# Macaron block on one core: a scratch field cleared behind each scatter of routed rows, TensorE's expert numbers as steps of their own, and newly written orders

## The reference, cut to what matters

```python
x = x + 0.5 * int8_linear(layernorm(x))             # quantised by token, weight int8
x = x + griffin_block(layernorm(x))                 # rmsnorm, conv, RG-LRU scan, gate; then a gated FFN of 512
x = x + 0.5 * int8_linear(layernorm(x))
x = x + 0.5 * moe(layernorm(x))                     # shared expert + top 2 of 8 experts, inner size 256
x = x + gated_linear_attention(layernorm(x))        # state 128x128 a sequence
x = x + 0.5 * moe(layernorm(x))                     # the same weights

def moe(x):                                         # expert: (silu(x Wg) * (x Wu)) Wd
    scores, idx = top_k(sigmoid(x Wr + rb), 2)
    out = shared(x)
    for e in range(8): out += cw[..., e] * expert_e(x)
```

## Time and profile before

| | |
|---|---|
| runs, us | 683.24, 683.96, 685.11 (median 683.96) |
| span of the profiled execution, us | 692.3 |
| mean granted clock of TensorE | 0.972 |
| instructions | 14370 |
| busy, us | PE 600.1, PEld 476.3, DVE 497.2, ACT 387.7, POOL 419.3 |
| POOL's scatters (L840) | 128.1 us in 128 |
| POOL's tile stores (L1132) | 96.3 us in 98 and 43.7 us in 44 |

### The profile page before, as it was taken

How to read it: one execution, slowest core, us unless ns; L and a number is a source line. 1 busy time by engine, 2 the same in 40 slices (tenths; PEclk the granted TensorE clock), 3 DMA queues, 4 the chain that set the end, 5 groups by cost and what they waited for, 6 DMA issues and landing times.

```text
span 692.3 us, 14370 instructions
## 1 busy us (share of the span) xinstructions
PE 600.1 (87%) x4124; PEld 476.3 (69%) x4124; DVE 497.2 (72%) x1721; ACT 387.7 (56%) x1019; POOL 419.3 (61%) x445
## 2 busy tenths in 40 slices
PE   0366999999989998999897899999999999978974
PEld 0224565655666797888696686769879989857863
DVE  7997999978998865557224798989877766553335
ACT  2395968988766545444353728466565355533541
POOL 5276696488567777567643614553776575775552
PEclk9996999999999999999999999999999999999997
DMA  7999000001033355666768600124216556566796
GB/s 258 410 411 371 0 1 1 1 0 32 13 99 94 97 156 161 186 193 180 211 176 245 235 6 1 35 66 131 74 43 172 153 151 177 161 182 189 231 297 232
DMA packets 60125, 100.97 MB, mean 146 GB/s; under 512 B 10288, under 2 KB 28592, under 8 KB 59792
## 3 DMA queue, kind: packets, MB, share of 16 engines
q1 hardware_dynamic: 50832, 81.52, 38.5%
q0 software_dynamic: 8640, 17.84, 7.4%
q10 hardware_dynamic: 576, 0.69, 0.3%
HBM read 61.79 MB, written 38.23 MB: 144 GB/s over the span
## 4 chain that ended last, share of the span: by engine, by line
PE 43%; DVE 13%; DMA 9%; issue 6%; POOL 3%; SPq 2%; ACT 2%; POOLq 0%; DVEq 0%; ACTq 0%
PE bank L1083 13%; PE bank L1058 6%; PE bank L1296 5%; DMA tin<-rows_by_expert 3%; PE bank L969 3%; PE bank L955 3%; PE bank L944 2%; DMA hid<-rows_done 2%; DMA rows_done<-tout,tdst 2%; PE bank L1064 2%; DMA rows_done<-tout,tin 1%; POOL rows_by_expert L840 1%; DVE qt L417 1%; PE bank L312 1%; PE bank L307 1%
## 5 line engine op out<-in xcount | busy, mean ns | idle before, releaser
L840 POOL DMA_INDIRECT rows_by_expert<-xx,sidx x128 | 128.1, 1001 | 72.2 <-issue 34.0
L1083 PE MATMUL bank<-tint,twt 128*128 128x128 f32 x1136 | 151.8, 282 | 6.0 <-DVE thidt L1121 3.4
L1083 PEld LDWEIGHTS bank<-tint,twt 128*128 128x128 f32 x1136 | 141.1, 196 | 22.0 <-issue 12.3
L1132 POOL DMA_INDIRECT rows_done<-tout,tin x98 | 96.3, 983 | 57.5 <-ACT tout L1107 34.8
L1121 DVE TENSOR_TENSOR thidt<-tsil,bank 128x256 f32<-128x256 f32 x142 | 58.2, 418 | 95.8 <-ACT tsil L1099 74.1
L1099 ACT ACTIVATE tsil<-bank 128x256 f32<-128x256 f32 x142 | 53.9, 384 | 89.9 <-PE bank L1083 88.4
L1058 PE MATMUL bank<-e_dn,thidt 128*128 x568 | 90.6, 286 | 15.5 <-DVE thidt L1121 7.3
L1058 PEld LDWEIGHTS bank<-e_dn,thidt 128*128 128x128 f32 x568 | 76.8, 195 | 25.2 <-issue 24.8
L1107 ACT ACTIVATE tout<-bank,tin 128x128 f32<-128x128 f32 x142 | 50.2, 366 | 62.9 <-PE bank L1064 43.7
L1132 POOL DMA_INDIRECT rows_done<-tout,tdst x44 | 43.7, 993 | 49.0 <-ACT tout L1107 35.9
L1296 PEld LDWEIGHTS bank<-bufA,bufB 128*127 128x127 f32 (+6 forms) x448 | 47.7, 176 | 11.6 <-issue 6.7
(11 more groups left out here) (272 smaller groups left out, 1331.0 us busy)
## 6 DMA issues: line engine op xcount, KB each, us to landing
twt<-moe_gu SPq DMA_DIRECT2D x142, 256.0 KB
rows_by_expert<-tout SPq DMA_DIRECT2D x25, 715.0 KB, 20.0
tin<-rows_by_expert SPq DMA_DIRECT2D x142, 65.0 KB, 2.6
hid<-rows_done SPq DMA_DIRECT2D x12, 512.0 KB, 5.5
x<-x_in SPq DMA_DIRECT2D x8, 256.0 KB, 4.4
rows_by_expert<-xx,sidx POOLq DMA_INDIRECT x128
out<-x SPq DMA_DIRECT2D x8, 256.0 KB, 3.9
rows_done<-tout,tin POOLq DMA_INDIRECT x98
```

The lines of the kernel that those rows point to most:

```text
L840: pool.indirect_dma_start(out=rows_by_expert, out_offset=bass.IndirectOffsetOnAxis(ap=sidx[h][:, k:k + 1], axis=0), in_=xx[h][:, r, t, :], ...
L1083: m = pe.matmul(bank[UP_BANKS[p][j]][:, c * P:(c + 1) * P], weights[:, c * P:(c + 1) * P], tint[g % TURNS][:, :], start=True, stop=True)
L1132: pool.indirect_dma_start(out=rows_done, out_offset=bass.IndirectOffsetOnAxis(ap=dst, axis=0), in_=tout[:, g % RING, :], in_offset=None).t ...
```

## The change

Three things. First, a scratch tile `pause` of 128 x 112 floats is cleared behind each of the 128 scatters, and POOL waits for the end of that; there is nothing of the kind behind the 142 tile stores. Second, the wait for the table and the register reads of TensorE leave `x_io_tensor` and become a step `x_ids_tensor`, called 38 times. Third, the five orders are written anew; apart from `x_ids_tensor` they have the same steps as before (sync 315, vector 636, gpsimd 293, scalar 745, tensor 704 and now 742).

```diff
 LEVELS = 7
+PAUSE = 112
 PIECES = 3
...
         tdst = sb("tdst", [P, RING], I32)
+        pause = sb("pause", [P, PAUSE])
         tout = sb("tout", [P, RING, P])
...
                     ap=sidx[h][:, k:k + 1], axis=0), in_=xx[h][:, r, t, :], in_offset=None).then_inc(s_scat[h], 16)
+                pool_step(pool, pool.memset(pause[:, :], 0.0))
 
 
...
+        def x_ids_tensor(pe, p, j):
+            pe.wait_ge(s_table, WAVES * p + wave_of(j) + 1)
+            expert_pe.update(values_of(ENG.PE, etab[p], chunk_at(j), E_ROUTED))
+
...
             if s >= LAG_DOWN:
                 j = s - LAG_DOWN
                 g = p * NT + j
-                if chunk_at(j):
-                    pe.wait_ge(s_table, WAVES * p + wave_of(j) + 1)
-                    expert_pe.update(values_of(ENG.PE, etab[p], chunk_at(j), E_ROUTED))
                 pe.wait_ge(s_thid, g + 1)
                 for c in range(IJ):
                     m = pe.matmul(bank[b][:, P:2 * P], thidt[g % TURNS][:, c, :], e_dn[:, expert_pe[j], c, :],
```

POOL's order at the start:

```diff
             k_first_gpsimd(pool)
             q_root1_gpsimd(pool, 0)
             q_root1_gpsimd(pool, 1)
+            k_split_gpsimd(pool)
             q_bias_gpsimd(pool, 0, 0)
-            k_split_gpsimd(pool)
             q_bias_gpsimd(pool, 1, 0)
             f_root_gpsimd(pool, 0)
             q_root_gpsimd(pool, 1, 0)
+            f_rstd_gpsimd(pool, 0)
             q_root_gpsimd(pool, 2, 0)
+            f_apply_gpsimd(pool, 1)
             q_bias_gpsimd(pool, 2, 0)
             q_bias_gpsimd(pool, 3, 0)
-            f_rstd_gpsimd(pool, 0)
-            f_apply_gpsimd(pool, 1)
             f_apply_gpsimd(pool, 0)
+            q_bias_gpsimd(pool, 4, 0)
             f_b_gpsimd(pool, 0)
             f_root_gpsimd(pool, 1)
             f_b_gpsimd(pool, 1)
+            f_root2_gpsimd(pool, 0)
...
```

DVE's order at the start:

```diff
             q_mom1_vector(dve, 0)
             q_stats_vector(dve, 1, 0)
             q_limits_vector(dve, 1, 0)
-            q_mom1_vector(dve, 1)
             q_par1_vector(dve, 0)
             q_scale_vector(dve, 0, 0)
             k_first_vector(dve)
+            q_whole_vector(dve, 0, 0)
+            q_mom1_vector(dve, 1)
+            q_limits_vector(dve, 3, 0)
+            q_stats_vector(dve, 2, 0)
             q_par1_vector(dve, 1)
+            k_decay_vector(dve)
             q_scale_vector(dve, 1, 0)
-            q_whole_vector(dve, 0, 0)
+            q_out_vector(dve, 0, 0)
             q_whole_vector(dve, 1, 0)
+            q_stats_vector(dve, 3, 0)
             q_limits_vector(dve, 2, 0)
-            q_limits_vector(dve, 3, 0)
-            q_out_vector(dve, 0, 0)
-            q_stats_vector(dve, 3, 0)
             f_stats_vector(dve, 0)
-            q_stats_vector(dve, 2, 0)
             q_out_vector(dve, 1, 0)
+            q_stats_vector(dve, 4, 0)
             f_stats_vector(dve, 1)
...
```

SP's order at the end:

```diff
+            for j in range(69, 71):
                 t_load_sync(sp_, 1, j)
-            t_weights_sync(sp_, 1, 66)
+            for j in range(68, 71):
+                t_weights_sync(sp_, 1, j)
             t_stored_sync(sp_, 1, 0)
             c_fetch_sync(sp_, 0, 1)
-            for j in range(68, 71):
-                t_load_sync(sp_, 1, j)
-            for j in range(67, 70):
-                t_weights_sync(sp_, 1, j)
             c_fetch_sync(sp_, 1, 1)
             c_fetch_sync(sp_, 2, 1)
-            t_weights_sync(sp_, 1, 70)
             c_fetch_sync(sp_, 3, 1)
             c_fetch_sync(sp_, 4, 1)
             c_fetch_sync(sp_, 5, 1)
             t_stored_sync(sp_, 1, 6)
             c_fetch_sync(sp_, 6, 1)
+            t_stored_sync(sp_, 1, 7)
+            c_fetch_sync(sp_, 7, 1)
             o_store_sync(sp_, 0)
             o_store_sync(sp_, 1)
             o_store_sync(sp_, 2)
-            t_stored_sync(sp_, 1, 7)
-            c_fetch_sync(sp_, 7, 1)
             o_store_sync(sp_, 3)
             o_store_sync(sp_, 4)
             o_store_sync(sp_, 5)
...
```

TensorE's order around the first tile of pass 1's last wave (an excerpt; `x_io_tensor(1, 49)` transposes it):

```diff
             x_up_tensor(pe, 1, 44)
-            x_io_tensor(pe, 1, 48)
+            e_gate_tensor(pe, 7, 1, 0)
+            x_ids_tensor(pe, 1, 41)
             x_up_tensor(pe, 1, 45)
-            x_io_tensor(pe, 1, 49)
+            for j in range(46, 49):
+                x_io_tensor(pe, 1, j)
             x_up_tensor(pe, 1, 46)
-            x_io_tensor(pe, 1, 50)
+            x_ids_tensor(pe, 1, 45)
+            e_up_tensor(pe, 7, 1, 0)
+            x_ids_tensor(pe, 1, 49)
             x_up_tensor(pe, 1, 47)
+            for j in range(49, 51):
+                x_io_tensor(pe, 1, j)
+            for j in range(48, 50):
...
```

More of the change, by code:

```diff
@@ L1534, in _ @@
                 t_load_sync(sp_, 0, j)
-            for j in range(31, 36):
+            for j in range(32, 35):
                 t_weights_sync(sp_, 0, j)
@@ L1555, in _ @@
                 t_load_sync(sp_, 0, j)
-            for j in range(47, 51):
+            for j in range(47, 49):
                 t_weights_sync(sp_, 0, j)
@@ L1659, in _ @@
             for j in range(44, 47):
                 t_load_sync(sp_, 1, j)
-            for j in range(41, 45):
+            for j in range(43, 48):
                 t_weights_sync(sp_, 1, j)
@@ L2448, in _ @@
             g_bias_gpsimd(pool, 1)
-            for j in range(65, 67):
-                t_store_gpsimd(pool, 0, j)
             g_root_gpsimd(pool, 1)
@@ L2455, in _ @@
             g_root_gpsimd(pool, 2)
+            for j in range(64, 67):
+                t_store_gpsimd(pool, 0, j)
             r_scatter_gpsimd(pool, 0, 1, 0)
@@ new lines, in _ @@
+            x_io_tensor(pe, 0, 24)
+            r_counts_tensor(pe, 6, 0)
+            e_up_tensor(pe, 5, 0, 0)
+            e_gate_tensor(pe, 5, 0, 1)
+            e_up_tensor(pe, 5, 0, 1)
+            for j in range(23, 25):
+                x_up_tensor(pe, 0, j)
+            x_io_tensor(pe, 0, 25)
+            e_down_tensor(pe, 5, 0)
+            r_turn_tensor(pe, 7, 0)
+            x_ids_tensor(pe, 0, 21)
+            x_ids_tensor(pe, 0, 25)
+            x_io_tensor(pe, 0, 26)
+            r_logits_tensor(pe, 7, 0)
@@ new lines, in _ @@
+            x_io_tensor(pe, 0, 39)
+            e_down_tensor(pe, 6, 0)
+            x_up_tensor(pe, 0, 39)
+            for j in range(40, 43):
+                x_io_tensor(pe, 0, j)
+            x_up_tensor(pe, 0, 40)
+            e_gate_tensor(pe, 7, 0, 0)
+            e_up_tensor(pe, 7, 0, 0)
+            x_io_tensor(pe, 0, 43)
+            x_up_tensor(pe, 0, 41)
+            x_ids_tensor(pe, 0, 53)
+            for j in range(42, 44):
+                x_up_tensor(pe, 0, j)
+            x_io_tensor(pe, 0, 44)
@@ L3107, in _ @@
             e_down_tensor(pe, 5, 1)
+            x_ids_tensor(pe, 1, 29)
             x_up_tensor(pe, 1, 27)
-            x_io_tensor(pe, 1, 29)
+            for j in range(29, 31):
+                x_io_tensor(pe, 1, j)
             r_turn_tensor(pe, 6, 1)
@@ new lines, in _ @@
+            x_up_tensor(pe, 1, 63)
+            for j in range(65, 67):
+                x_io_tensor(pe, 1, j)
+            x_up_tensor(pe, 1, 64)
+            x_ids_tensor(pe, 1, 65)
+            for j in range(67, 69):
+                x_io_tensor(pe, 1, j)
+            for j in range(65, 67):
+                x_up_tensor(pe, 1, j)
+            x_io_tensor(pe, 1, 69)
+            x_up_tensor(pe, 1, 67)
+            for j in range(70, 72):
+                x_io_tensor(pe, 1, j)
+            x_up_tensor(pe, 1, 68)
@@ L3589, in _ @@
-            x_in_scalar(act, 0, 67)
+            for j in range(53, 55):
+                x_out_scalar(act, 0, j)
+            x_silu_scalar(act, 0, 56)
+            x_in_scalar(act, 0, 59)
+            for j in range(55, 57):
+                x_out_scalar(act, 0, j)
+            for j in range(60, 62):
+                x_in_scalar(act, 0, j)
+            for j in range(57, 60):
+                x_silu_scalar(act, 0, j)
+            x_out_scalar(act, 0, 57)
+            for j in range(62, 65):
+                x_in_scalar(act, 0, j)
```

2001 lines of the change are left out of this document (982 added, 1019 removed).

## The result

The changed kernel takes 703.8 us (median of 4 runs, 703.16 to 705.52) against 683.6 before: ratio 1.0295, 95% interval 1.0275 to 1.0315, 20 us slower. I had forecast 686.5 with a range up to 698. The direction was right, the size was not.

What follows compares the result with a forecast made beforehand. TensorE, busy 87% of the span, was taken as the bound, with POOL nearly full where waves wait for scatters. Start -4.5, pass 0 +8.5, register loads -2.5, pass 1 +4.6, end -3.5 gave +2.6 us: 686.5, range 675 to 698.

Steps and rivals of the forecast that it cites:

- start: First 62 us: apply(1) fills POOL's idle stretch and b(0) comes earlier, -4.5 us (bounds -5.8 and -1).
- pause, pass 0: Units 2 to 7 of pass 0: 0.30 us per scatter, 0.61 before a store, 17.7 us before absorption.
- pause, pass 1: Units 6 and 7 of pass 1: pauses plus one store, less 0.3 idle, +4.6 us (bounds +1 and +7).
- new order in pass 0: Units 2 to 7: two more tile stores ahead of POOL's last scatter, 1.26 us each, +2.5.
- register loads: Chunk heads on PE: expert-number reads come earlier, behind matmuls already queued, -2.5 us (bounds 0 and -6).
- end: Last tiles: all loads issued first and c_adds put behind x_hid(70), -3.5 us (bounds -5 and -1).
- Of this the 10.0 us of idle time is absorbed: Pass 0, units 2 to 7: POOL's idle time takes up 10.0 of 20.2 us added; +8.5 reaches the last wave.
- elsewhere the pause costs nothing: Units 0, 1 of pass 0 and 0 to 5 of pass 1: POOL idles while PE works, so no cost.
- signs named ahead: In the new trace: scatters 1.56 us start to start, unit 7's last at about 339, PE idle time growing.
- cheap pause (0.08): POOL's scatters: the 0.30 gap overlaps the memset, pause nearly free, start and end pay; 675.6 us, chance 0.31.
- half price: POOL's scatters: 0.20 us each, pass 0 +5, pass 1 +3.5; 682 to 684 us, chance 0.13.
- fourth rival: Register loads still stop PE's queue, the next engine holds the start (-1); sum +8.6, 692.5 us, chance 0.07.

Runs made afterwards that it cites:

- e6: Kernel before with the new order only up to the first scatter of unit 0 (some 155 us), no pause: 683.39 us, ratio 0.9962.
- e5: Kernel before with the pause added behind the 64 scatters of pass 0 only: 695.4 us, ratio 1.0164.
- e11: Kernel before with the pause added behind the 64 scatters of pass 1 only: 690.15 us, ratio 1.0086.
- e7: Kernel before with the new order only from some 155 to 430 us (pass 0), no pause: 696.84 us, ratio 1.0167.
- e2: Changed kernel without the pause's memset and its wait; new orders and register steps stay: 699.77 us, ratio 1.0236.
- e8: Kernel before with the new order only from some 628 us to the end, no pause: 683.74 us, ratio 0.9967.
- e4: Changed kernel with TensorE's register reads put back into x_io, pause and orders kept: 707.44 us, ratio 1.0336.
- e1: Kernel before, unchanged, run again for a second trace: 684.88 us, ratio 1.0016.
- e3: Kernel before with only the pause added behind all 128 scatters: 705.65 us, ratio 1.0310.
- e9: New order in pass 0 only, no pause, with the last wave's table moved behind x_hid(0, 33) on DVE: 691.89 us, ratio 1.0113.

## Why the prediction was wrong, step by step

| step of the sum | forecast | measured on the 684 us chips |
|---|---|---|
| start | -4.5 | -2.6 (-0.5 to -4.7), e6 |
| pause, pass 0 | +6.0 (8.5 less two stores) | +11.2 (7.9 to 14.5), e5 |
| pause, pass 1 | some +5 | +5.9 (3.8 to 8.0), e11 |
| new order in pass 0 | +2.5 (two stores) | +11.4 (8.6 to 14.4), e7 |
| new order in pass 1 | some -0.5 | some +10 (2 to 18) if the parts add, what e2 leaves over e6, e7 and e8; not run alone |
| register loads | -2.5 | not settled, e4 |
| end | -3.5 | -2.3 (-0.2 to -4.3), e8 |
| all | +2.6 | +20 |

Two steps failed.

**The first is "Of this the 10.0 us of idle time is absorbed".** It was wrong twice. The 10.0 came from one slow execution; the second trace has 5.1 (e1). And that idle time was not room for more work: in e3 POOL's line of work grew by 12.7 us, its idle time beyond the fixed gaps stayed (5.1 and 5.6 us), and the stretch grew by 13.0. The reading that fits is that POOL, the ring of slots, the loads and PE form a loop. Without the absorption my own price per pause would have given 17.7 in pass 0; the true one gives 12.7 for the old order, and by e5 11.2 of that is in the time.

**The second is what I gave no price**: the rewritten middle of the orders. I compared the place of each x_io in PE's work and found it the same within some 5 us, and let "apart from two stores" stand for nothing. That comparison doesn't see what stands ahead of a short step on another engine. All new orders and register steps together were forecast at -8.5 us (-4.5, +2.5, -0.5, -2.5, -3.5) and cost 16 without the pause (e2). The table of the last wave, 6 us of DVE, moved from behind x_hid(34) to ahead of x_hid(30), which cost 3.7 us (e9, 0 to 7). Of the rest of pass 0's 11.4, the wait for tile 65's load (3.2 us against 0.8) is the longest single wait in the trace and was not tested; pass 1's share was not found on a chip where it counts. e2's trace has one candidate there: PE waits 5.05 us at 621.3 for a thidt behind the last table of pass 1, which in the old order stands one x_hid later.

**Where it was right.** The start gained by the mechanism named: apply(1) fills POOL's idle stretch (36.58 in the changed kernel), b(0) starts at 49.66 instead of 53.13, and mix(0) waits 1.24 us at 55.12 instead of 5.77 at 56.47. At mix(0) itself 1.3 us show, for DVE is the next to be late, as feared; in the changed kernel unit 7's FFN ends at 226.7 us, where e1 has 226.2, and in e6 the first tile's transposition is 0.8 us earlier than in e1 (208.00 against 208.79). So the median's 2.6 is only in part followed through the trace. POOL's timeline there:
```profile
36.58 3.14 POOL L621 TENSOR_SCALAR h<-x,lf_mean,lf_rstd 128x128 f32<-128x128 f32 x4
...
49.66 1.45 POOL L591 TENSOR_TENSOR bufB<-bufD,bufB 128x512 f32<-128x512 f32 x1
```
The end gained as described: the c_add at 682.88 waits for nothing (5.45 us before). Pass 1's pause came out near its price, but not where I had it: "elsewhere the pause costs nothing" is wrong, since e11 lost some 4.4 us before the last waves begin. The sign of the whole was partly luck: the pause cost less on top of the new orders than I had for it, and the orders, forecast as a gain, cost 16.

**The pause's price and the two halves don't add.** On the old order the pause costs 21 us, on the new one 4 (-3 to 11, e2 to the changed kernel). POOL's stretch from unit 2 to unit 7 shows how this comes about in pass 0:

| kernel | stretch | POOL idle beyond the fixed gaps |
|---|---|---|
| e1, old order | 122.0 | 5.1 |
| e3, old order and pause | 135.0 | 5.6 |
| e2, new order | 132.5 | 13.4 |
| changed, new order and pause | 138.6 | 5.2 |

In e2 the new order holds PE elsewhere, and POOL waits up to 5.29 us at a time. The pause adds some 14 us to POOL there and the stretch grows by 6.1: the rest fills idle time that was there because what POOL waits for was late for another reason. In e1, e3 and the changed kernel POOL is down to some 5 us, and this last part took up nothing. So absorption does exist, but the idle time in the trace of the kernel before was not of that kind. By these traces the order's loss in this stretch is hidden under POOL's in the changed kernel, and either alone would have lengthened it by 10 us or more.

**Slips in the sum.** Of the 48 pauses in it the last stands behind unit 7's last scatter: 47 pauses and nine stores behind one lie ahead of it, which is 0.61 less. And start, loads and end give back 4.5 + 2.5 + 3.5 = 10.5, not 10.9. Neither changes the outcome. Of the signs named ahead, start to start was 1.45 us instead of 1.56, the last scatter of unit 7 came at 342.6 instead of 339, and PE's idle time in the stretch did grow, from 3.9 us in e1 to 14.4.

**The rivals.** The cheap pause (0.08) did not happen, nor the half price as I meant it: at 0.19 a scatter I had 682 to 684, and the missing absorption and the unpriced orders kept this from coming true. The memset does not block DVE: DVE was busy 495.9 us in e3 against 496.7 in e1. The fill was rarely held either: of 128 the median is 0.206 us, the longest 0.494 in the changed kernel and 1.285 in e3. The rule of the Trainium skill, GPSIMD Engine Reference, section 8 (Key points), that GpSimd and VectorE share SBUF interfaces, shows no cost here for such a fill. Of the fourth rival the half that says "a start moved on paper is held by the next engine" came true in part.

## What to carry to other kernels

Before idle time of an engine is counted as room for more work, ask what that engine waits for: if it waits for something that its own output releases, the added time can go through one to one, as it did here on the old order. Take such a figure from two traces, above all where the traced execution is slower than the runs. In a rewritten order, look on every engine for long steps that now stand ahead of a short one that TensorE needs; the place of the matmuls in TensorE's own list doesn't show them.

## What the runs showed that was not expected

- The sign of this change depends on the chip: ratio 1.0295 (1.0275 to 1.0315) where before takes 684 us, 0.9655 (0.9593 to 0.9717) where it takes 803. The instructions are the same; the granted clock and TensorE's idle time are not.
- The drops of TensorE's clock at 278.1 and 346.4 (first trace of before) and at 311.9 (e7) last 3.4 us each; at half speed that is, as an estimate, 1.7 us of matmuls. In the first trace of before these two drops more went with a lag behind e1 of 8.6 us by tile 60 and 7.8 at the first tile of pass 1. What began the lag is not shown: it was 2.5 us at tile 20 (274.4 against 271.9), ahead of the first of them, and 4.8 at tile 24 (284.5 against 279.7).
- A tile store behind a waited memset starts 0.83 us late, a scatter 0.28. Ahead of a store's DMA stand a wait and a semaphore increment (`t_store_gpsimd`), and so they do ahead of the first scatter of a unit; that of unit 3 starts 0.84 behind the pause (217.60 in the changed kernel) and 0.30 behind another scatter in the same order without it (215.38 in e2). Stores behind another DMA mostly start after 0.30 as well. So the wait and the increment seem to be hidden behind a DMA and not behind a waited compute instruction; no run took them out.
